# Order of products, sum buffers and small vector operations in the last pass of a four-layer graph network

## The reference

```
h = (x @ W.T).reshape(N, H, C)
e = leaky_relu(a_s[src] + a_d[dst], 0.2)
m = segment_max(e, dst);  p = exp(e - m[dst])
denom = segment_sum(p, dst)
out = segment_sum((p / (denom[dst] + 1e-16))[:, :, None] * h[src], dst)
out = elu(out.reshape(N, H * C) + bias) + x
x = layernorm(x + out)
```

## Time and profile before

| | |
|---|---|
| median of 3 runs | 5779.85 us (5770.6 to 5787.17) |
| the profiled execution | 5752.64 us, span 5750.9 us |
| busy, share of the span | PE 74%, DVE 64%, ACT 34%, POOL 63% |
| last pass, first and last L1882 | 5144.3 and 5735.2 us |
| last pass, busy in 5400 to 5500 | PE 71.7, DVE 84.9, ACT 66.2, POOL 83.5 us; DMA share 0.97, 350 GB/s; granted clock 0.88 |

### The profile page before, as it was taken

One profiled execution on the slowest core, in us unless ns is written; L12 is line 12 of the kernel. 1 busy time (PEld: TensorE's weight loads), 2 busy tenths in 40 slices (PEclk: granted clock), 3 DMA queues, 4 the chain that ended last, 5 costly groups with the idle time before them and its releaser, 6 DMA issues. The chain is left out here.

```text
span 5750.9 us, 69994 instructions
## 1 busy us (share of the span) xinstructions
PE 4250.1 (74%) x16758; PEld 2855.9 (50%) x16758; DVE 3705.5 (64%) x10203; ACT 1959.4 (34%) x3345; POOL 3618.8 (63%) x3319
## 2 busy tenths in 40 slices
PE   2377679999999999999999777767777400026776
PEld 1255445556666666666666566656666300012222
DVE  1255456566666666666666566668888645558887
ACT  0011145532222222222222222227777300016666
POOL 7488644433556666555555566657777776668887
PEclk7688889999999999999999887778999755559888
DMA  9988799984433333333333233339999522249997
GB/s 378 283 154 153 139 303 365 363 313 148 142 121 123 123 123 123 122 121 119 118 119 111 90 124 122 123 119 317 325 325 324 197 88 81 86 137 352 350 347 286
DMA packets 497174, 1129.62 MB, mean 196 GB/s; under 512 B 164006, under 2 KB 246906, under 8 KB 497030
## 3 DMA queue, kind: packets, MB, share of 16 engines
q1 hardware_dynamic: 331530, 866.20, 43.1%
q0 software_dynamic: 113184, 174.84, 12.5%
q10 hardware_dynamic: 52316, 87.06, 4.3%
HBM read 627.40 MB, written 543.83 MB: 204 GB/s over the span
## 5 line engine op out<-in xcount | busy, mean ns | idle before, releaser
L1067 PE MATMUL psum<-W2b,arena 128*128 128x256 f32 x3136 | 725.2, 379 | 0.0
L799 DVE TENSOR_SCALAR arena<-arena 128x256 f32<-128x256 f32 x784 | 463.0, 653 | 369.4 <-POOL arena L794 364.9
L1048 PE MATMUL psum<-arena,W1b 128*128 128x512 f32 x1568 | 699.1, 599 | 0.0
L1067 PEld LDWEIGHTS psum<-W2b,arena 128*128 128x128 f32 x3136 | 573.1, 190 | 66.3 <-issue 0.5
L1761 PE MATMUL psum<-arena,ident 128*128 128x512 f32 x784 | 418.8, 685 | 194.7 <-POOL arena L1819 192.4
L959 ACT ACTIVATE arena<-psum,hbias 128x512 f32<-128x512 f32 x392 | 269.5, 687 | 809.6 <-PE psum L1048 809.6
L1192 POOL DMA_INDIRECT tab<-arena,IDX x392 | 408.9, 1043 | 190.4 <-issue 114.0
L1610 POOL DMA_INDIRECT ad_d<-arena,FE x392 | 406.9, 1038 | 156.1 <-issue 127.4
L1048 PEld LDWEIGHTS psum<-arena,W1b 128*128 128x128 f32 x1568 | 289.8, 190 | 402.4 <-issue 402.4
L790 POOL TENSOR_TENSOR arena<-arena,lneps 128x4 f32<-128x4 f32 x196 | 42.0, 215 | 668.3 <-DVE arena L786 667.5
L1251 PE MATMUL psum<-ident,arena 128*128 128x128 f32 x24 | 5.7, 424 | 590.4 <-DVE arena L1419 581.1
(11 more groups left out here) (256 smaller groups left out, 9269.0 us busy)
## 6 DMA issues: line engine op xcount, KB each, us to landing
arena<-tab SPq DMA_DIRECT2D x194, 544.0 KB
arena<-x_d SPq DMA_DIRECT2D x202, 512.0 KB
arena<-in_x SPq DMA_DIRECT2D x194, 512.0 KB
x_d<-arena SPq DMA_DIRECT2D x194, 512.0 KB
tab<-zero SPq DMA_DIRECT2D x11, 5832.0 KB
tab<-blank SPq DMA_DIRECT2D x97, 544.0 KB
h_d<-arena SPq DMA_DIRECT2D x97, 528.0 KB
arena<-h_d SPq DMA_DIRECT2D x97, 528.0 KB
```

What stands on the lines that cost most here:

```text
L799: v.tensor_scalar(y[:, j, :], r[:, j, :], self.mv[:, j, 0:1], self.rs[:, j:j + 1], ALU.subtract, ALU.mult).then_inc(self.s["y"], 1)
L1048: last = pe.matmul(psum[:, HB[c], :], W1b[:, f, c * P:(c + 1) * P], x1T[:, f, :], start=False, stop=(f == FH - 1))
L1067: last = pe.matmul(outB(j), hid[:, c, j * P:(j + 1) * P], W2b[:, c, :], start=(c == 0), stop=(c == KH - 1))
```

## The change

TensorE's loops are exchanged: the two matmul calls on `oh` (one for each bank) come first and wait for `oh` alone; then it waits for `oS` and does the two on `oS`. `rr` has four buffers in place of two: the sum of beat k waits for the normalized rows of k-4, not of k-2. VectorE's `factors` is cut into `heads` (L1851's addition, with its waits for `ht` and `tt`), `slopes`, `maxima` and `below`; `shares` into `sums`, `totals` and `shares`. The list of an even beat k is now: elu(k), neg(k-1), `heads(k+4)`, rr(k), `slopes(k+4)`, statistics(k), `maxima(k+4)`, memset and aggregates(k), `below(k+4)`. Of an odd beat: elu(k), neg(k-1), rr(k), `sums(k+3)`, statistics(k), `totals(k+3)`, memset and aggregates(k), `shares(k+3)` (reciprocal and last product). A wait for GpSimd's L1825 of beat k-2 stands before the memset. GpSimd's, ScalarE's and SyncE's lists are as before, but for the index of `rr`.

```diff
-            rr = take([2, J, D])
+            rr = take([NB, J, D])
...
-                    pe.wait_ge(r["oS"], k.s + 1)
-                    pe.wait_ge(r["oh"], k.s + 1)
                     wait(pe, r["r"], k.s + Z - NB + 1)
-                    for i in range(2):
-                        for n, a in enumerate((oh, oS)):
+                    for n, (a, made) in enumerate(((oh, "oh"), (oS, "oS"))):
+                        pe.wait_ge(r[made], k.s + 1)
+                        for i in range(2):
                             last = pe.matmul(psum[:, b + i, :], ident[:, :], a[...],
                                              start=(n == 0), stop=(n == 1))
...
+                def heads(k):
                     for n in (k, k.plus(1)):
                         b = n.slot(NB)
                         v.wait_ge(gd[b], 16 * (n.turn(NB) + GD[b] + 1))
                         v.wait_ge(n_t[b], 16 * (n.turn(NB) + 2 * USES[b] + 1))
                     v.tensor_tensor(out=l1, in0=pair_cols(ht, k, D), in1=pair_cols(ht, k, D + H), op=ALU.add).then_inc(r["small"], 1)
...
+                def negated(k):
+                    b = k.slot(2)
+                    v.wait_ge(r["mv"], J * (k.s + Z + 1))
+                    wait(v, r["nm"], k.s + ZP - 1)
+                    v.tensor_scalar(neg[:, b, :], mv[:, b, :, 0], -1.0, None, ALU.mult).then_inc(r["neg"], 1)
...
                 def body(k):
-                    b = k.slot(2)
+                    b, b4 = k.slot(2), k.slot(NB)
+                    even = b == 0 and live(k.plus(4), NS)
+                    odd = b == 1 and live(k.plus(3), NS)
                     v.wait_ge(r["ex"], k.s + Z + 1)
                     v.scalar_tensor_tensor(out=banks(k), in0=ex[:, b, :, :], scalar=-1.0, in1=banks(k), op0=ALU.add, op1=ALU.max).then_inc(r["elu"], 1)
+                    if not (k.known() and k.s == 0):
+                        negated(k.plus(-1))
+                    if even:
+                        heads(k.plus(4))
...
-                    wait(v, r["y"], J * (k.s + Z - 1))
-                    v.scalar_tensor_tensor(out=rr[:, b, :, :], in0=xt[:, k.slot(NB), :, :], scalar=2.0, in1=banks(k), op0=ALU.mult, op1=ALU.add).then_inc(r["r"], 1)
+                    wait(v, r["y"], J * (k.s + Z - NB + 1))
+                    v.scalar_tensor_tensor(out=rr[:, b4, :, :], in0=xt[:, b4, :, :], scalar=2.0, in1=banks(k), op0=ALU.mult, op1=ALU.add).then_inc(r["r"], 1)
+                    if even:
+                        slopes(k.plus(4))
+                    elif odd:
+                        sums(k.plus(3))
...
+                    if even:
+                        maxima(k.plus(4))
+                    elif odd:
+                        totals(k.plus(3))
+                    v.wait_ge(r["ve"], k.s + ZP - 1)
                     v.wait_ge(r["st"], J * (k.s + Z + 1))
                     v.memset(gap, 0.0)
                     for j in range(J):
                         v.bn_aggr(mv[:, b, j, :], st[:, j, :]).then_inc(r["mv"], 1)
-                    v.wait_ge(r["mv"], J * (k.s + Z + 1))
-                    wait(v, r["nm"], k.s + ZP - 1)
-                    v.tensor_scalar(neg[:, b, :], mv[:, b, :, 0], -1.0, None, ALU.mult).then_inc(r["neg"], 1)
-                    if b == 0 and live(k.plus(4), NS):
-                        factors(k.plus(4))
-                    elif b == 1 and live(k.plus(3), NS):
+                    if even:
+                        below(k.plus(4))
+                    elif odd:
                         shares(k.plus(3))
                 run_beats(v, NS, body, NB)
+                negated(beat(NS - 1, NB))
```

More of the change, by code:

```diff
@@ L1786, in normed @@
                     for j in range(J):
-                        act.activation(y[:, k.slot(NB), j, :], rr[:, b, j, :], ACT.Identity, bias=nm[:, b, j:j + 1], scale=rsd[:, b, j:j + 1]).then_inc(r["y"], 1)
+                        act.activation(y[:, k.slot(NB), j, :], rr[:, k.slot(NB), j, :], ACT.Identity, bias=nm[:, b, j:j + 1], scale=rsd[:, b, j:j + 1]).then_inc(r["y"], 1)
                 def store(k):
@@ L1841, in l_vector @@
             def l_vector(v):
-                def factors(k):
-                    p = k.turn(2)
-                    c0 = 6 * p
+                def heads(k):
                     for n in (k, k.plus(1)):
@@ L1849, in factors, with slopes @@
                         v.wait_ge(n_t[b], 16 * (n.turn(NB) + 2 * USES[b] + 1))
-                    M = pair_cols(tt, k, MC)
                     v.tensor_tensor(out=l1, in0=pair_cols(ht, k, D), in1=pair_cols(ht, k, D + H), op=ALU.add).then_inc(r["small"], 1)
-                    v.wait_ge(r["small"], c0 + 1)
+                def slopes(k):
+                    v.wait_ge(r["small"], 6 * k.turn(2) + 1)
                     v.scalar_tensor_tensor(out=es, in0=l1, scalar=SLOPE, in1=l1, op0=ALU.mult, op1=ALU.max).then_inc(r["small"], 1)
-                    v.wait_ge(r["small"], c0 + 2)
@@ L1855, in factors, with maxima, below @@
-                    v.tensor_tensor(out=top, in0=M, in1=es, op=ALU.max).then_inc(r["small"], 1)
-                    v.wait_ge(r["small"], c0 + 3)
+                def maxima(k):
+                    v.wait_ge(r["small"], 6 * k.turn(2) + 2)
+                    v.tensor_tensor(out=top, in0=pair_cols(tt, k, MC), in1=es, op=ALU.max).then_inc(r["small"], 1)
+                def below(k):
+                    p = k.turn(2)
+                    v.wait_ge(r["small"], 6 * p + 3)
                     wait(v, r["w"], p)
-                    v.tensor_tensor(out=dd[:, 0, :, :], in0=M, in1=top, op=ALU.subtract).then_inc(r["d"], 1)
+                    v.tensor_tensor(out=dd[:, 0, :, :], in0=pair_cols(tt, k, MC), in1=top, op=ALU.subtract).then_inc(r["d"], 1)
@@ L1859, in factors, with sums @@
                     v.tensor_tensor(out=dd[:, 1, :, :], in0=es, in1=top, op=ALU.subtract).then_inc(r["d"], 1)
-                def shares(k):
[L1862 to L1868, removed]
+                def sums(k):
+                    v.wait_ge(r["w"], k.turn(2) + 1)
+                    v.tensor_tensor(out=t1, in0=pair_cols(tt, k, SC), in1=ww[:, 0, :, :], op=ALU.mult).then_inc(r["small"], 1)
@@ L1869, in shares, with totals @@
+                def totals(k):
+                    v.wait_ge(r["small"], 6 * k.turn(2) + 4)
+                    v.scalar_tensor_tensor(out=den, in0=t1, scalar=1e-16, in1=ww[:, 1, :, :], op0=ALU.add, op1=ALU.add).then_inc(r["small"], 1)
+                def shares(k):
+                    v.wait_ge(r["small"], 6 * k.turn(2) + 5)
                     v.reciprocal(den, den).then_inc(r["small"], 1)
-                    v.wait_ge(r["small"], c0 + 6)
+                    v.wait_ge(r["small"], 6 * k.turn(2) + 6)
@@ L1873, in shares @@
                                     in1=den.rearrange("p (a j) h -> p a (j h)", a=1).to_broadcast([P, 2, 2 * J * H]), op=ALU.mult).then_inc(r["cc"], 1)
+                def negated(k):
[3 more added lines that the diff above has]
+                    v.tensor_scalar(neg[:, b, :], mv[:, b, :, 0], -1.0, None, ALU.mult).then_inc(r["neg"], 1)
                 for s in (0, 2):
-                    factors(beat(s, NB))
-                    shares(beat(s, NB))
+                    for part in (heads, slopes, maxima, below, sums, totals, shares):
+                        part(beat(s, NB))
                 def body(k):
-                    b = k.slot(2)
+                    b, b4 = k.slot(2), k.slot(NB)
+                    even = b == 0 and live(k.plus(4), NS)
+                    odd = b == 1 and live(k.plus(3), NS)
                     v.wait_ge(r["ex"], k.s + Z + 1)
                     v.scalar_tensor_tensor(out=banks(k), in0=ex[:, b, :, :], scalar=-1.0, in1=banks(k), op0=ALU.add, op1=ALU.max).then_inc(r["elu"], 1)
+                    if not (k.known() and k.s == 0):
+                        negated(k.plus(-1))
+                    if even:
+                        heads(k.plus(4))
                     v.wait_ge(r["elu"], k.s + 2 * Z + 1)
-                    v.wait_ge(n_x[k.slot(NB)], 16 * (k.turn(NB) + 2 * USES[k.slot(NB)] + 1))
-                    wait(v, r["y"], J * (k.s + Z - 1))
-                    v.scalar_tensor_tensor(out=rr[:, b, :, :], in0=xt[:, k.slot(NB), :, :], scalar=2.0, in1=banks(k), op0=ALU.mult, op1=ALU.add).then_inc(r["r"], 1)
+                    v.wait_ge(n_x[b4], 16 * (k.turn(NB) + 2 * USES[b4] + 1))
+                    wait(v, r["y"], J * (k.s + Z - NB + 1))
[4 more added lines that the diff above has]
+                        sums(k.plus(3))
                     v.wait_ge(r["r"], k.s + Z + 1)
@@ L1889, in body @@
                     for j in range(J):
-                        v.bn_stats(st[:, j, :], rr[:, b, j, :]).then_inc(r["st"], 1)
+                        v.bn_stats(st[:, j, :], rr[:, b4, j, :]).then_inc(r["st"], 1)
+                    if even:
[3 more added lines that the diff above has]
+                    v.wait_ge(r["ve"], k.s + ZP - 1)
                     v.wait_ge(r["st"], J * (k.s + Z + 1))
```

## The result

The changed kernel takes 5896.33 us (median of 6, 5885.87 to 5899.18), the kernel before 5781.83 (median of 6): ratio 1.0196, 95% interval 1.0181 to 1.0210. It is about 2% slower, well clear of the noise. Forecast was 5888.

A forecast was written before the change was run, and what follows sets the result against it. A compute chain over three beats set the beat, with the DMA close behind. Even 7.9 plus odd 6.6 gives a pair of 14.5 us, 2.3 more; 47 x 2.3 = 108 on 5752.6 is 5861, plus 27 is 5888; range 5805 to 5965.

The forecast's parts named there:

- L: Time from issue to landing of the `tab` load that `heads` waits for: taken as 4.7 us, between 4.07 and 6.48.
- The odd beat: VectorE from neg to neg: `sums` blocked until 2.2 and `totals` until 4.1 by GpSimd's products, end at 6.6 us.
- collisions: VectorE's two-SBUF-input small operations held until GpSimd's running product ends, 1.84 us instead of 0.19; the prediction says ports.
- The even beat: On VectorE `heads` waits until 2.3 after the neg, `slopes` is blocked until 4.1, whole beat 7.9 us.
- flat 14.5: Pair of beats in the last pass: with the block, any L from 4.07 to 4.8 gives 14.5 us.
- the early wait: VectorE's `heads`, straight behind the neg of k-1, waits for two tables: 2.3 us in each of 47 pairs, 108 us.
- Ports only, 5808: Rival: tables come in time, only GpSimd's products block VectorE's small operations; pair 12.8, +28 us, chance 0.10.
- Worth nothing here: TensorE's new order: 1.85 us less from the products' end to the exp's end, costed at nothing in the changed kernel.
- The cover that it named: The elu that needs the products begins 9 us after their end, still 7.3 with a pair of 12.8 us.
- the DMA's cap: A beat moves 2.146 MB, 5.88 us at 365 GB/s, 0.21 less than before: at most -21 us over 98 beats.
- faster rival: Rival: the chain gets shorter, `heads` finds its tables, gain counts until the DMA is full; -21 us, 5759, chance 0.07.
- The buffers' 16.4 us: Four buffers remove VectorE's wait for the normalized rows of k-2, 16.4 us at most; gain taken to lie inside the stall.

The follow-up runs named there:

- b1: a2 with only `sums` and `totals` moved to the changed kernel's places in the odd beat: 5771.44 us, 1.0028 of the kernel before.
- b4: b1 with `sums` and `totals` replaced in the loop by statistics with one SBUF input, denominators not recomputed: 5735.07 us, 0.9962 of the kernel before.
- d2: a2 with only a wait for the rows and tables of k+4 and k+5 behind the even beat's elu: 5677.13 us, 1.0137 of the kernel before.
- a2: The kernel before with TensorE's loops exchanged, four buffers of sums and the wait they need: 5724.15 us, 0.9946 of the kernel before.
- b3: The changed kernel with the neg back right behind the aggregates of its own beat: 5852.68 us, 1.0168 of the kernel before.
- b2: a2 with only the neg of k-1 put behind elu(k): 5775.45 us, 1.0031 of the kernel before.
- a3: The changed kernel with `heads`, `slopes`, `maxima` and `below` all at the even beat's end: 5766.72 us, 1.0020 of the kernel before.
- c1: The changed kernel with TensorE's old loops and both waits first: 5729.65 us, 1.0231 of the kernel before.
- a1: The kernel before with only TensorE's loops exchanged, heads' product first: 5726.67 us, 0.9952 of the kernel before.
- c0: The changed kernel run again, unaltered, as the base for c1 on its chip: 5711.87 us, 1.0200 of the kernel before.

## Why the prediction was right

*The position of the issue and the landing.* The sum said: table issued 4.2 behind the neg, L = 4.7, `heads` ready 2.3 after its own neg. The pair above shows 4.22, 4.63 and 2.29; the means over 5200 to 5800 are 4.23, 5.0 and 2.9. Taking L below the 6.48 of the earlier trace rows was the step that carried the size. That 6.48 was a late one of its kind: a landing shows only where VectorE waits for it, in the kernel before in 8 of 41 pairs from 5200 to 5700, each 6.5 to 6.8 us behind the issue. In the others the tables were there by then, so the typical L before isn't known, and how much of the fall is the DMA's emptying isn't either.

*The odd beat.* Blocked until 2.2 and 4.1, end at 6.6. Measured 2.25, 4.10 and 6.56 in the pair shown; half of the odd beats take 6.2, the mean is 6.39. b1 and b4 show that the collisions do this.

*The even beat.* 7.9 forecast, and no beat took that: they take 7.26 or 8.5 and more, 8.35 on average; in the pair shown it was 8.52 and the whole 15.1. One term was wrong in it: I let `heads` pass in 0.19 and `slopes` be blocked for 0.3. As `heads` is released in the middle of GpSimd's products it is itself the one to be blocked (mean 0.90, here 1.84), and `slopes` mostly goes free (0.31). So the sum of residuals comes behind the second product and not beside it, which the forecast had end at 3.8, and a released `heads` costs in steps, where I had a flat 14.5. Against it, small operations that are dealt out start with hardly a gap, some 0.1 us less each than I had put down. That the whole pass comes to 14.50 a pair, the forecast to the digit, is in part luck: the steady beats of 5200 to 5800 give 8.35 + 6.39 = 14.7, the pass's ends less, and the errors of the two beats have opposite signs.

*Which of the causes is the cost.* The prediction gave nearly all to the early wait, and 28 us to the ports alone. d2 has the wait without the collisions: +1.9% over a2. From there the rest adds little: with the small operations dealt out it is b3, 1.0168, +0.3%, and with the late neg the changed kernel, 1.0196, +0.3% more. Without the early wait, b1 has collisions by dealt-out `sums`, +0.8% over a2, and b2 by the late neg, +0.85%. These two don't add: together they are a3, 1.0020, no more than either alone. The late neg moves the products, and the mean of `sums` in a3 is 1.07 us in place of the 1.79 of b1; summed over its small operations a pair is stretched by some 1.6 us in b1, 1.3 in b2 and 1.7 in a3, and the pairs are 12.6 us in all three. Taking the early group away (a3) gives back 0.0196 - 0.0020 = 1.8%.

*Ports only, 5808.* The nearest kernel is a3: 5766.72 where the kernel before takes 5755.32, +11 and not +28. That doesn't show the rival over-priced: over a2, which has the new order, a3 is 0.74% or 43 us slower, and order and buffers together had gained 31 us, which the prediction had put at nothing. Nor is a3 the rival itself, as its `slopes` and `maxima` stand elsewhere.

*The products' order and the buffers.* "Worth nothing here" was wrong by 18 us (c1), by a way that the prediction didn't have: the table lands later, not the elu. The cover that it named was there: the products that end at 5411.31 are used by the elu of 5421.03, 9.7 us later. Alone the order is worth -28 us, more than the -21 that the DMA's cap allowed. Of the faster rival this one part was sound, a shorter path until the DMA is full, and it needs VectorE's list as it was. The buffers' 16.4 us came to nothing, as the order alone had taken that wait away.

a2 beats both kernels: 0.9946 of the kernel before. It is the change without its third part, and a1, the order alone, can't be told from it.

## What to carry to other kernels

Before moving an operation forward, list what its waits wait for and hold the distance from that transfer's issue against the landing time that the trace shows under load; here the wait moved, and the operation of 0.19 us only came with it (d2). A trace shows a landing only where something waited for it, so look at the waits that are missing as well. Small operations with two SBUF inputs cost, in this kernel, the rest of the GpSimd product that they meet, and nothing beside its short instructions. A busy share of 85% on VectorE didn't mean that its idle time could be filled; look at what runs on the neighbour in that time.

## What the runs showed of the hardware that I had not expected

The landing time of a 544 KB load varies from beat to beat, from 4.0 to 7.1 us at a DMA share of 0.85, by more than its mean moved between the kernels in which nearly every table was waited for (4.83 in c0, 4.87 in b3, 5.0 in the changed kernel, 5.29 in d2, 5.36 in c1, all at shares of 0.85 to 0.89). VectorE's small operations beside GpSimd's power, an instruction of 1.0 us on 128x4 elements (L1828), keep their 0.19 in the kernel before, though it reads SBUF too; only the 1.9 us products were seen to block them. The products themselves lost nothing to VectorE: 3.76 us a pair of them in every timeline shown. TensorE's granted clock over 5200 to 5650 was 0.90 in the kernel before and 0.93 in a1, though its matmuls of a beat now come in two halves with a wait between; in the changed kernel, with the same two halves in longer beats, it was 0.82 over 5200 to 5800. What moved the clock no run takes apart.
